# A fused stack of transformer layers on one core: the chosen-token layers with another product order, half the table gather, the values' bias at a copy, a down map with slots on partitions, and stage joins that go half by half

## The reference: what is computed

```python
scores = jnp.einsum('btd,d->bt', hidden_states, w_router)
_, idx = jax.lax.top_k(scores, k)            # k = 128 of 1024 tokens
x = sel.reshape(S, D); pos = idx.reshape(S)
h = _rms_norm(x, ln1_w)
q = (h @ wq + bq)...; kk = (h @ wk + bk)...; v = (h @ wv + bv)...
q = q * cos + _rotate_half(q) * sin          # cos, sin of the token's position
att = softmax(causal(q kk / sqrt(128)))      # 16 heads, 8 of keys and values
x1 = x + (att v) @ wo
h2 = _rms_norm(x1, ln2_w)
processed = x1 + silu(h2 @ w_gate) * (h2 @ w_up) @ w_down
gate = jax.nn.sigmoid(sel_scores)
output = hidden_states.at[b, idx].set(gate * processed + (1 - gate) * x)
```

## Time and profile before

| what | value |
|---|---|
| median of 3 runs | 1580.17 us (1577.37 to 1586.71) |
| the profiled execution's own time | 1579.09 us |
| its span (first to last instruction) | 1577.9 us |
| PE, DVE, ACT, POOL busy | 93%, 73%, 65%, 43% of the span |
| mean granted clock of PE | 0.974 of full |
| share of PE in the chain that ended last | 64% (ACT 16%, DVE 16%) |

### The profile page before, as it was taken

One profiled execution on the slowest core, in us unless ns is written; L12 is line 12 of the kernel. 1 busy time (PEld: TensorE's weight loads), 2 busy tenths in 40 slices (PEclk: granted clock), 3 DMA queues, 4 the chain that ended last, 5 costly groups with the idle time before them and its releaser, 6 DMA issues.

```text
span 1577.9 us, 23638 instructions
## 1 busy us (share of the span) xinstructions
PE 1464.7 (93%) x8378; PEld 1222.1 (77%) x8378; DVE 1144.6 (73%) x2615; ACT 1023.2 (65%) x2246; POOL 681.5 (43%) x802
## 2 busy tenths in 40 slices
PE   6999999999999998898999999999998977978898
PEld 5778888888888886775888888888885865655576
DVE  6888898989898975646675766666666649777646
ACT  4898988888898986353665655655553436463654
POOL 4657666676756563042433333333320411722223
PEclk8999999999999999899999999999999998997999
DMA  2000000000000001501000000000006013000000
GB/s 84 11 1 1 18 1 17 1 18 18 1 7 1 8 1 36 233 1 48 21 21 7 23 25 8 28 21 14 1 7 245 24 62 126 1 0 0 1 0 27
DMA packets 14201, 46.17 MB, mean 29 GB/s; under 512 B 3074, under 2 KB 3074, under 8 KB 11652
## 3 DMA queue, kind: packets, MB, share of 16 engines
q1 hardware_dynamic: 14084, 44.66, 7.8%
HBM read 43.60 MB, written 1.05 MB: 28 GB/s over the span
## 4 chain that ended last, share of the span: by engine, by line
PE 64%; ACT 16%; DVE 16%; issue 3%; POOL 1%; DMA 0%; SPq 0%; DVEq 0%; ACTq 0%; POOLq 0%
PE ps L142 26%; PE ps L337 13%; PE ps L1126 8%; PE ps L326 7%; ACT a_pT_hi L385 4%; ACT a_prob L353 3%; ACT a_o_two L625 3%; PE ps L1865 2%; PE ps L1871 2%; DVE a_prob L346 2%; DVE a_pT_lo L393 2%; ACT a_q L615 1%; PE ps L1867 1%; PE ps L1881 1%; PE ps L1884 1%
## 5 line engine op out<-in xcount | busy, mean ns | idle before, releaser
L368 POOL TENSOR_SCALAR a_prob<-a_prob,a_rowinv 128x128 f32<-128x128 f32 (+7 forms) x256 | 189.1, 752 | 163.6 <-DVE a_rowinv L362 163.6
L353 ACT ACTIVATE a_prob<-a_prob,a_negmax 128x128 f32<-128x128 f32 (+7 forms) x256 | 198.3, 780 | 32.4 <-DVE a_negmax L346 30.9
L393 DVE TENSOR_TENSOR a_pT_lo<-ps,a_pT_hi 128x512 fp32r<-128x512 f32 (+3 forms) x384 | 193.1, 550 | 20.3 <-ACT a_pT_hi L385 17.6
L368 POOL TENSOR_SCALAR b_prob<-b_prob,b_rowinv 128x128 f32<-128x128 f32 (+7 forms) x128 | 94.6, 752 | 234.2 <-DVE b_rowinv L362 234.2
L346 DVE CUSTOM_DVE_ANT_0 a_prob<-ps,a_mask 128x128 f32<-128x128 f32 (+7 forms) x256 | 187.2, 749 | 9.0 <-PE ps L142 8.6
L385 ACT ACTIVATE a_pT_hi<-ps 128x512 fp32r<-128x512 f32 (+3 forms) x384 | 164.6, 492 | 22.8 <-PE ps L326 10.4
L326 PE MATMUL ps<-ident,a_prob 128*128 128x128 f32 x1152 | 156.3, 277 | 8.1 <-DVE a_pT_lo L393 5.9
L353 ACT ACTIVATE b_prob<-b_prob,b_negmax 128x128 f32<-128x128 f32 (+7 forms) x128 | 99.7, 779 | 82.4 <-DVE b_negmax L346 82.1
L326 PEld LDWEIGHTS ps<-ident,a_prob 128*128 128x128 f32 x1152 | 130.1, 141 | 26.8 <-issue 10.8
L142 PE MATMUL ps<-a_k_hi,a_q 128*128 128x512 f32 (+3 forms) x384 | 140.9, 373 | 7.6 <-DVE a_negmax L346 7.5
L337 PE MATMUL ps<-a_pT_hi,a_v 128*128 128x512 f32 (+3 forms) x384 | 132.6, 352 | 1.7 <-DVE a_q L655 0.7
(11 more groups left out here) (447 smaller groups left out, 4145.9 us busy)
## 6 DMA issues: line engine op xcount, KB each, us to landing
f_wq<-in_f_wq SPq DMA_DIRECT2D x2, 2048.0 KB, 10.2
f_wo<-in_f_wo SPq DMA_DIRECT2D x2, 2048.0 KB, 18.5
b_w_raw<-in_b_qk SPq DMA_DIRECT2D x16, 256.0 KB, 2.7
a_w_raw<-in_a_w SPq DMA_DIRECT2D x8, 384.0 KB, 3.3
a_o_raw<-in_a_o SPq DMA_DIRECT2D x8, 256.0 KB, 2.6
f_rope<-in_f_rope SPq DMA_DIRECT2D x2, 1024.0 KB, 4.9
f_wk<-in_f_wk SPq DMA_DIRECT2D x2, 1024.0 KB, 12.3
f_wv<-in_f_wv SPq DMA_DIRECT2D x2, 1024.0 KB, 14.3
```

The lines of the kernel that those rows point to most:

```text
L353: act.activation(prob, prob, ACT.Exp, bias=a.negmax[:, n:n + 1], scale=-1.0, accum_out=a.rowsum[:, n:n + 1]).then_inc(*g.exped.mark(a.tag, u))
L368: pool.tensor_scalar(prob, prob, a.rowinv[:, n:n + 1], 1.0, ALU.mult, ALU.mult).then_inc(*g.normed.mark(a.tag, u))
L393: dve.tensor_tensor(lo, src, fr(hi), ALU.subtract).then_inc(*g.lo.mark(a.tag, u, j0 // 4))
```

## The change

In the stages "f1" and "f2":

- `ended` is no longer called by PE. PE waits, half by half, for the additions to `g.x` (`tokens_ready`). The same holds at the start of "b" and of layer 1. The order of the "out" jobs in both attention stages is half outside, tile inside. The router's weights `g.f_wr` are loaded once, in stage "a".
- Front: the order of PE's products becomes raw(0), var(0), var(1), raw(1), inv(0), inv(1), turn_h(0), s_col(0), turn_h(1), s_col(1); ACT and DVE follow.
- Rank: after the nine products of a key tile, PE runs three (`F_SPIN`) bf16 products of 512 columns into bank 7, which nobody reads.
- The table holds cosines and sines in one tile of 128 rows: 8 products in place of 16; DVE makes `f.ropes` of it with four operations of 64 rows.
- "own" goes behind map 1 on PE and behind `turn(1)` on DVE, "others" behind map 3, `mask` behind `turn(3)`.
- The bias of the values is added where ACT copies the weighed values out (`weighed`, now two operations of 256 columns with a bias each); the two products with `f.bv` go.
- "xs" is split in halves, one behind `scores(2)`, one behind `scores(3)`. The transposes of `f.take` and the gate product (now one column) go behind `turn_prob(1)`. `warm_act` goes behind `weighed(3)`.
- The down map puts the slots on partitions (8 products of 256 columns), and `f.ch` is added into the same bank by two products with the identity before it; ACT copies the sum out with the gate as its scale. The two DVE operations and PE's transposes go.

```diff
+
+def tokens_ready(g, e, b):
+
+    for sig, event in g.tokens[b]:
+        e.wait_ge(*sig.at(*event))
...
+        else:
+            tokens_ready(g, pe, b)
...
-        a.outs = [("out", gr, m, qb) for gr in range(A_KV) for m in range(KT) for qb in range(NH2)]
...
+        a.outs = [("out", gr, m, qb) for gr in range(A_KV) for qb in range(NH2) for m in range(KT)]
...
+    sp.dma_start(g.f_wr[:], g.ins["f_wr"]).then_inc(*g.f_loaded["wr"].mark(by=16))
...
-    ended(g, pe)
...
+F_SPIN = 3
...
-        f.wr, f.rope, f.ln = sb("wr", [P, KT]), sb("rope", [P, TT, 2, P]), sb("ln", [P, 2, KT])
-        f.bqk, f.bq, f.bv = sb("bqk", [P, F_QK]), sb("bq", [P, F_HEADS]), sb("bv", [1, F_KV * F_HD])
+        f.rope, f.ln = sb("rope", [P, TT, P]), sb("ln", [P, 2, KT])
+        f.bqk, f.bq, f.bv = sb("bqk", [P, F_QK]), sb("bq", [P, F_HEADS]), sb("bv", [P, F_KV])
...
+        g.tokens = [[(g.f_dve, (tag, "x", m, b)) for m in range(KT)] for b in range(NH2)]
...
+    def raw(b):
+        for k in range(KT):
+            pe.wait_ge(*dve.at(tag, "cen", b, k))
+            t = mm(bank[4 * b + 3], f.wrb[:, k], f.h[:, k, b * HALF:(b + 1) * HALF], k == 0, k == KT - 1)
+        t.then_inc(*done.mark(tag, "raw", b))
+
+    def var(b):
+        pe.wait_ge(*dve.at(tag, "squares", b))
+        for j in range(HT):
+            t = mm(bank[4 * b + 1][:, j:j + 1], f.sq[:, b, 0, j * P:j * P + P], g.avg[:, 0:1], True, True)
+        t.then_inc(*done.mark(tag, "var", b))
+
+    def inv(b):
+        pe.wait_ge(*dve.at(tag, "diag", b))
+        mm(bank[4 * b + 2], g.ones[:], f.ndiag[:, b], True, True).then_inc(*done.mark(tag, "inv", b))
+
+    def s_col(b):
+        pe.wait_ge(*dve.at(tag, "s", b))
+        for j in range(HT):
+            t = pe.transpose(bank[4 * b + 3][:, j * P:j * P + P], f.s[:, (HT * b + j) * P:(HT * b + j + 1) * P], g.ident[:])
+        t.then_inc(*done.mark(tag, "s_col", b))
+
     for b, cc in halves():
+        tokens_ready(g, pe, b)
         for k in range(KT):
             t = mm(bank[4 * b], g.avg[:], g.x[:, k, cc], k == 0, k == KT - 1)
         t.then_inc(*done.mark(tag, "mean", b))
     pe.wait_ge(*dve.at(tag, "wrb"))
-    for b, cc in halves():
-        for k in range(KT):
-            pe.wait_ge(*dve.at(tag, "cen", b, k))
-            t = mm(bank[4 * b + 3], f.wrb[:, k], f.h[:, k, cc], k == 0, k == KT - 1)
-        t.then_inc(*done.mark(tag, "raw", b))
-        pe.wait_ge(*dve.at(tag, "squares", b))
-        for j in range(HT):
-            t = mm(bank[4 * b + 1][:, j:j + 1], f.sq[:, b, 0, j * P:j * P + P], g.avg[:, 0:1], True, True)
-        t.then_inc(*done.mark(tag, "var", b))
+    raw(0)
+    var(0)
+    var(1)
+    raw(1)
+    inv(0)
+    inv(1)
     turn_h(0)
+    s_col(0)
     turn_h(1)
-    for b in range(NH2):
-        pe.wait_ge(*dve.at(tag, "diag", b))
-        mm(bank[4 * b + 2], g.ones[:], f.ndiag[:, b], True, True).then_inc(*done.mark(tag, "inv", b))
-    for b in range(NH2):
-        pe.wait_ge(*dve.at(tag, "s", b))
-        for j in range(HT):
-            t = pe.transpose(bank[4 * b + 1][:, j * P:j * P + P], f.s[:, (HT * b + j) * P:(HT * b + j + 1) * P], g.ident[:])
-        t.then_inc(*done.mark(tag, "s_col", b))
+    s_col(1)
...
-    t.then_inc(*done.mark(tag, "rank"))
+        if j == TT - 1:
+            t.then_inc(*done.mark(tag, "rank"))
+        for n in range(F_SPIN):
+            mm(bank[7], f.ident_b[:], f.beats[j // 4][:, j % 4, 0:HALF], True, True)
...
-    for m in range(2):
-        for c in range(TT):
-            t = mm(bank[6][:, m * P:m * P + P], f.rope[:, c, m], f.take[:, c], c == 0, c == TT - 1)
+    for c in range(TT):
+        t = mm(bank[6][:, 0:P], f.rope[:, c], f.take[:, c], c == 0, c == TT - 1)
...
-        if p == 0:
+        if p == 1:
             for c in range(TT):
                 t = mm(bank[5][:, 0:1], f.take[:, c], f.place[:, c:c + 1], c == 0, c == TT - 1)
             t.then_inc(*done.mark(tag, "own"))
-        if p == 2:
+        if p == 3:
...
-            mm(bank[1 + c], f.h1[:, k], f.wv[:, k, cc], k == 0, False)
-        mm(bank[1 + c], g.ones[0:1, :], f.bv[0:1, cc], False, True).then_inc(*done.mark(tag, "v", c))
+            t = mm(bank[1 + c], f.h1[:, k], f.wv[:, k, cc], k == 0, k == KT - 1)
+        t.then_inc(*done.mark(tag, "v", c))
...
+    pe.wait_ge(*g.f_loaded["wv"].at(tag))
     pe.wait_ge(*act.at(tag, "qk", 3))
     values(0)
     scores(1)
     pe.wait_ge(*act.at(tag, "qk", 4))
     values(1)
-    scores(2)
-    for c in range(TT):
-        for m in range(KT):
-            t = mm(bank[0][:, m * P:m * P + P], f.h_tok[:, c, m * P:m * P + P], f.take[:, c], c == m == 0, c == TT - 1)
-    t.then_inc(*done.mark(tag, "xs"))
-    scores(3)
-    pe.wait_ge(*act.at(tag, "qk", 5))
-    pe.wait_ge(*act.at(tag, "xs"))
-    for k in range(KT):
-        t = mm(bank[3][:, 0:P], f.wrb[:, k], f.xs[:, k], k == 0, k == KT - 1)
-    t.then_inc(*done.mark(tag, "gate"))
-    for b in range(2):
-        pe.wait_ge(*act.at(tag, "v", b))
-        for j in range(4):
-            t = pe.transpose(bank[1 + b][:, j * P:j * P + P], f.take[:, 4 * b + j], g.ident[:])
-        t.then_inc(*done.mark(tag, "takeT", b))
-
...
-    pe.wait_ge(*g.f_loaded["wo"].at(tag))
+    def own_tokens(half):
+
+        for c in range(4 * half, 4 * half + 4):
+            for m in range(KT):
+                t = mm(bank[0][:, m * P:m * P + P], f.h_tok[:, c, m * P:m * P + P], f.take[:, c], c == m == 0, c == TT - 1)
+        return t
+
+    def turn_take(b):
+        pe.wait_ge(*act.at(tag, "v", b))
+        for j in range(4):
+            t = pe.transpose(bank[1 + b][:, j * P:j * P + P], f.take[:, 4 * b + j], g.ident[:])
+        t.then_inc(*done.mark(tag, "takeT", b))
+
+    scores(2)
+    own_tokens(0)
+    scores(3)
+    own_tokens(1).then_inc(*done.mark(tag, "xs"))
     turn_prob(0)
     turn_prob(1)
+    turn_take(0)
+    turn_take(1)
+    pe.wait_ge(*act.at(tag, "qk", 5))
+    pe.wait_ge(*act.at(tag, "xs"))
...
+    for k in range(KT):
+        t = mm(bank[3][:, 0:1], f.xs[:, k], g.f_wr[:, k:k + 1], k == 0, k == KT - 1)
+    t.then_inc(*done.mark(tag, "gate"))
+    pe.wait_ge(*g.f_loaded["wo"].at(tag))
...
+    pe.wait_ge(*pool.at(tag, "ch"))
+    for m in range(KT):
+        mm(bank[3][:, m * P:m * P + P], f.ch[:, m], g.ident[:], m == 0, False)
     for half in range(2):
         pe.wait_ge(*dve.at(tag, "hid", half))
         for i in range(4 * half, 4 * half + 4):
-            for m in range(KT):
-                t = mm(bank[3][:, m * P:m * P + P], f.wd[:, i, m * P:m * P + P], f.hid[:, i], i == m == 0, i == FI_T - 1)
-    t.then_inc(*done.mark(tag, "down"))
-    pe.wait_ge(*dve.at(tag, "ch"))
-    for m in range(KT):
-        t = pe.transpose(bank[0][:, m * P:m * P + P], f.ch[:, m], g.ident[:])
+            t = mm(bank[3][:, 0:D], f.hid[:, i], f.wd[:, i], False, i == FI_T - 1)
...
-    for b, cc in halves():
-        ht = slice(b * HT, b * HT + HT)
+    def raw(b):
         act.wait_ge(*pe.at(tag, "raw", b))
-        act.activation(f.s[:, cc], bank[4 * b + 3], ACT.Copy).then_inc(*done.mark(tag, "raw", b))
+        act.activation(f.s[:, b * HALF:(b + 1) * HALF], bank[4 * b + 3], ACT.Copy).then_inc(*done.mark(tag, "raw", b))
+
+    def std(b):
         act.wait_ge(*pe.at(tag, "var", b))
-        act.activation(f.std[:, ht], bank[4 * b + 1][:, 0:HT], ACT.Sqrt, bias=g.eps[:, 0:1]).then_inc(*done.mark(tag, "std", b))
+        act.activation(f.std[:, b * HT:b * HT + HT], bank[4 * b + 1][:, 0:HT], ACT.Sqrt, bias=g.eps[:, 0:1]).then_inc(*done.mark(tag, "std", b))
+
+    raw(0)
+    std(0)
+    std(1)
+    raw(1)
...
+
         act.wait_ge(*pe.at(tag, "o", n))
-        act.activation(f.oT[:, 4 * n:4 * n + 4].rearrange(FLAT), bank[4 + n], ACT.Copy).then_inc(*done.mark(tag, "oT", n))
+        for j in range(2):
+            hd = 4 * n + 2 * j
+            kv = hd * F_KV // F_HEADS
+            t = act.activation(f.oT[:, hd:hd + 2].rearrange(FLAT), bank[4 + n][:, 2 * j * P:(2 * j + 2) * P], ACT.Identity,
+                               bias=f.bv[:, kv:kv + 1])
+        t.then_inc(*done.mark(tag, "oT", n))
...
+    scores(2)
     act.wait_ge(*pe.at(tag, "xs"))
     act.activation(f.xs[:, :].rearrange(FLAT), bank[0][:, 0:2 * P], ACT.Copy).then_inc(*done.mark(tag, "xs"))
-    scores(2)
+    turned(0)
     scores(3)
-    warm_act(g, act, 1e-5)
-    turned(0)
     turned(1)
+    act.wait_ge(*g.f_loaded["bv"].at(tag))
     weighed(0)
     turned(2)
     weighed(1)
     turned(3)
     weighed(2)
     weighed(3)
+    warm_act(g, act, 1e-5)
...
-    act.activation(f.gate[:], bank[3][:, 0:P], ACT.Sigmoid).then_inc(*done.mark(tag, "gate"))
...
-    act.activation(f.chT[:], bank[0][:, 0:D], ACT.Copy).then_inc(*done.mark(tag, "chT"))
+    act.wait_ge(*done.at(tag, "gate"))
+    act.activation(f.chT[:], bank[3][:, 0:D], ACT.Copy, scale=f.gate[:]).then_inc(*done.mark(tag, "chT"))
...
-    dve.wait_ge(*g.f_loaded["wr"].at(tag))
```

(47 more changed lines are left out.)

22 lines of the change are left out of this document (9 added, 13 removed).

## The result

The changed kernel took 1556.61 us (median of 4 runs, 1549.69 to 1559.31) against 1578.77 us before (4 runs beside it, 1576.25 to 1586.71): a ratio of 0.9845, 95% interval 0.9815 to 0.9874, so about 1.5% faster (the quotient of the two medians is 0.986). The forecast was 1557.5. Of all executions in this document one was disturbed, the profiled one of `own_early` (2236 us at a mean granted clock of 0.584), and no reading uses it; without it that kernel's median is 1552.36. The profiled execution took 1559.31 us with a span of 1558.1, 19.8 us less than the span before; the sum had said 22.1.

A forecast was written before the change was run, and what follows sets the result against it. PE was taken to bound the kernel (93% busy, 64% of the chain), through its work, clock and waits. Gains of 13.6 us in f1 and 8.55 in f2, together 22.1, gave 1557.5 us, range 1550 to 1567.

The forecast's parts named there:

- Joins: Stage joins: PE takes the mean earlier; 2.4 us into f1, 1.0 out of it, 1.05 into f2, nothing into layer 1.
- Front: Mean's start to first comparison: new order lets roots and inverses run under raw(1); gain 1.1 us per stage, 0.5 to 1.5.
- Rank with spins: Rank of key tiles: each spin takes 0.23 us, a tile costs PE 0.05 more than DVE; cost 0.3 us per stage.
- B: Rival on the rank: spins don't hold the clock, cost double, and the gathers' gain is lost; 1568 us; chance 0.07.
- D: Rival on the rank: slower than before by the spins alone, if one costs 0.69 us or more; chance 0.03.
- Gather and table: h1 gather at full clock, 2.4 us in f1 and 1.3 in f2; 16 fewer table instructions, 1.8 us per stage.
- Maps to the output map: From map 0 on: new order of turns, scores and values takes 42.0 us; gain 3.9 us in f1, 2.3 in f2.
- The pause: Before scores(0): PE stands for about 2.5 us, waiting for four turns and the mask.
- Table load: Between scores and weighing: the load of 1.28 us, with no drain, goes off the chain and runs beside PE's products.
- Tail: Down map's end to the put: only the copy is left, 0.45 us; gain 1.3 us per stage.
- Rival A: The pause before scores(0) brings the clock down during scores and values, once or twice; 1559 to 1561 us; chance 0.25.
- E: Rival: joins and front are given back by transfers or GpSimd's splits in "b"; 6 us less gain, 1563 us; chance 0.08.

The follow-up runs named there:

- own_early: Changed kernel with own's operations before turn(1), the mask right behind turn(1), and "others" behind map 2: 1553.23 us, ratio 0.9829 to the kernel before.
- pe_waits: Changed kernel with PE waiting for both halves of the tokens before the first mean product of f1, b, f2 and layer 1: 1559.26 us, ratio 0.9884.
- no_spin: Changed kernel without the three bf16 products per key tile in the rank: 1560.19 us, ratio 0.9876 to the kernel before.
- spin_alone: Kernel before the change, with the three bf16 products per key tile as its only change: 1575.11 us, ratio 0.9959.
- warm_early: Changed kernel with the function table load put back between exp of scores(3) and the copy of the second transposed probabilities: 1559.71 us, ratio 0.9888.
- own_fill: The kernel of `own_early` plus fourteen products that nobody reads in PE's waits at the start of stage "b": 1554.04 us, ratio 0.9826.
- fill_b: Changed kernel plus fourteen products that nobody reads in PE's waits at the start of stage "b": 1555.45 us, ratio 0.9852.

## Why the prediction was right

The sum is what came, piece by piece but for the front, and no rival decided. With f1's front at full clock the pieces of the two stages would add up to 13.7 + 8.6 = 22.3, against 22.1. That the profiled span gained only 19.8 and the medians 22.2 depends on clock and layer 1 in the executions that were drawn, which the sum didn't treat. Of the 2.3 us by which the span gained less, the fronts are 2.6 and "b" 1.9; the rank (0.6), the maps (0.4) and layer 1 (1.3) gave more than taken.

- **Joins.** Sized right, each within 0.1, and `pe_waits` takes the 1.0 back. What PE did earlier ahead of layer 1 gained nothing, for the reason given: `l_taps` begins 6.5 us after the put's first product now, 6.3 before, and takes 3.57 us (chain of waits, f2 and the start of layer 1, changed kernel; answers to the earlier trace rows):

```profile
1269.87 3.71 PE ps L1137 x8
...
1276.39 3.57 DMA l_taps<-in_l_taps
```

- **Front.** This is the step that failed, by 2.6 us of the 22.1 (2.2 forecast for both stages, -0.4 measured): "inv(0) can begin at about 8.75 after the start, inv(1) lands at 10.5". At full clock (f2) it begins at 9.19 and both end near 11: PE runs the 16 instructions of var, raw(1) and both inv in one line, 5.49 us from 5.58 on, and I had let inv(0) begin before raw(1) was through. The sixteen transposes then stand in one line, so s_col(1) ends at 12.8, where the sum had 12.35. Gain 0.7, not 1.1. And in f1 there were 1.7 us more to lose, which no term had: clock 0.50 through raw(1), 3.66 us in place of 1.96.

```profile
628.05 1.95 PE L1137 MATMUL ps<-avg,f_sq 128*128 128x1 f32 x16 [0.26 <-DVE f_sq L1476]
629.85 3.66 PE L1137 MATMUL ps<-f_h,f_wrb 128*128 128x512 f32 x4
```

- **Rank with spins.** A spin is 0.21 us in the rank ((1.05 - 0.41)/3), 0.27 by its row, where 0.23 was taken. PE keeps DVE's beat of 1.05 and isn't late. `no_spin` and `spin_alone` show the mechanism from both sides, so B and D fall. (B's own price counted five late tiles, while the rank's term counts seven.)
- **Gather and table.** Right to 0.1 us. PE at half the clock counted as busy before, and that was the 2.5 us.
- **Maps to the output map.** Map 0 to x1 takes 41.92 against 42.0 in the sum, scores(0) at 15.44 against 15.3. Two errors inside cancel: own's two operations cost 1.36 where 0.45 was taken (0.16 and 0.29 before, 0.16 and 1.20 with POOL's addition beside them), and the turn behind them cost 0.97 less than 3.05, since POOL was idle then. The pause is 0.86 + 1.42, not one of 2.5.
- **Table load.** Hidden beside `out`, and it costs its duration once it is put back on the chain (`warm_early`).
- **Tail.** Right: 1.32 against 1.3. The put begins 0.55 us behind the down map (707.34 to 707.89).
- **Rival A** (clock down behind the pause) had 0.25: it shows nowhere. Over the ten traces with the changed order, the 20 pieces from scores(0) to x1 are 26.4 to 26.5 us, but for `warm_early` (27.7, the load) and `own_fill` (27.5, given back by the turns). **E** was right in one part: "b" became 1.9 us longer. But 1.7 of it is the clock, not transfers or GpSimd: the first eighteen instructions of b's maps take 4.54 us in place of 2.88, and 2.88 again in `fill_b`. Before, the low stretch was the 3 us of the product with `b_n_diag`; now it goes from about 718.7 to 729, over the same product (which takes as long at either place, 3.62 and 3.78) and the first of the maps' instructions, 0.43 us apart in place of 0.23 with 512 columns and 0.21 in place of 0.12 with 256:

```profile
727.58 0.63 PE L148 MATMUL ps<-b_h_lo,b_w_hi 128*128 128x512 f32 x1
...
729.25 0.28 PE L148 MATMUL ps<-b_wv_hi,b_h_lo 128*128 128x256 f32 x1
```

In `fill_b` this is gone; in `own_fill`, with the same fills, a short stretch is left (0.66 from 720 to 725). From b's mean to its first map product it is 0.46 longer than before (13.88 against 13.42), and 13.81 with `fill_b`, so this part isn't the clock's; it is open, and no larger than what lies between the kernel before and `spin_alone` (12.93), which have the same program there. Why the low stretch is longer after the change isn't settled: with the old joins (`pe_waits`) it was there too, with before's kernel plus spins it wasn't.
